# ScalarE's two output-side activations moved ahead of the next pair's two SiLUs, in every step of a hand-ordered Mamba-2 mixer

## The reference

```
x = x + block_sparse_linear(layernorm(x))
x = x + ffn(layernorm(x))        # gate/up/down weights dequantised from int4 values, SiLU gate
x = x + mamba2(layernorm(x))     # 128 heads of 64, state 128, 8 groups, chunks of 128
x = x + ffn(layernorm(x))
```

```
gate, hBC, dt = split(x @ in_proj_w.T)
hBC = silu(causal_conv4(hBC) + conv_b)            # x: 8192 channels, B and C: 1024 each
y   = ssm_scan(x, B, C, softplus(dt), A) + D * x
y   = y * rsqrt(mean(y*y) + eps) * norm_w * silu(gate)
out = y @ out_proj_w.T
```

## Time and profile before

| | |
|---|---|
| time, median of 3 runs | 2216.73 us (2215.08 to 2217.02) |
| the profiled execution, its own time | 2217.02 us |
| its span in the profile | 2215.3 us |
| mean granted TensorE clock | 0.982 of full speed |
| busy: TensorE, its weight loads | 96%, 79% of the span |
| busy: VectorE, ScalarE, GpSimd | 76%, 62%, 43% |

### The profile page before, as it was taken

One profiled execution on the slowest core, in us unless ns is written; L12 is line 12 of the kernel. 1 busy time (PEld: TensorE's weight loads), 2 busy tenths in 40 slices (PEclk: granted clock), 3 DMA queues, 4 the chain that ended last, 5 costly groups with the idle time before them and its releaser, 6 DMA issues. The chain is left out here.

```text
span 2215.3 us, 37449 instructions
## 1 busy us (share of the span) xinstructions
PE 2117.9 (96%) x13374; PEld 1740.4 (79%) x13374; DVE 1694.6 (76%) x2683; ACT 1378.9 (62%) x1872; POOL 944.2 (43%) x637
## 2 busy tenths in 40 slices
PE   5999976999999999999999999999999999859999
PEld 4788865788888888888888888888888888738887
DVE  8655566879888888878888888888888888665554
ACT  2222236787777877777787877777787777522221
POOL 2222222555454545454454555555454545342221
PEclk9999988999999999999999999999999999969999
DMA  4434313332323332333333333232333333333431
GB/s 166 131 128 169 105 59 100 98 113 93 118 91 111 101 106 99 109 97 109 97 108 97 109 97 114 92 118 87 112 98 103 103 107 98 119 110 118 170 140 68
DMA packets 128564, 241.89 MB, mean 109 GB/s; under 512 B 13968, under 2 KB 48528, under 8 KB 128144
## 3 DMA queue, kind: packets, MB, share of 16 engines
q1 hardware_dynamic: 128400, 239.73, 33.6%
HBM read 234.17 MB, written 5.51 MB: 108 GB/s over the span
## 5 line engine op out<-in xcount | busy, mean ns | idle before, releaser
L854 PE MATMUL ring<-m_lnt,w_sb 128*128 128x512 f32 x3456 | 857.3, 398 | 3.4 <-DVE xc L1196 3.4
L854 PEld LDWEIGHTS ring<-m_lnt,w_sb 128*128 128x128 f32 x3456 | 631.8, 189 | 127.9 <-DVE xc L1196 3.7
L1375 POOL TENSOR_TENSOR w_sb<-w_raw,w_sb 128x512 fp32r<-128x512 f32 x288 | 426.7, 1487 | 136.4 <-ACT w_sb L1050 136.1
L1390 POOL TENSOR_TENSOR ysq<-ysq,y 128x512 f32<-128x512 f32 x126 | 163.9, 1301 | 662.0 <-ACT y L1094 662.0
L951 PE MATMUL ring<-wo,ygs 128*128 128x512 f32 x1536 | 370.2, 390 | 2.2 <-POOL wo L1380 2.2
L951 PEld LDWEIGHTS ring<-wo,ygs 128*128 128x128 f32 x1536 | 287.7, 188 | 64.5 <-issue 4.3
L1196 DVE SCALAR_TENSOR_TENSOR xc<-ring,cw,xc 128x511 f32<-128x511 f32 (+2 forms) x384 | 286.1, 745 | 22.7 <-ACT xc L1062 13.6
L1380 POOL TENSOR_TENSOR wo<-wo_raw,wo 128x512 fp32r<-128x512 f32 x128 | 221.3, 1729 | 0.6 <-ACT wo L1106 0.6
L1050 ACT ACTIVATE w_sb<-w_raw 128x512 fp32r<-128x512 f32 x288 | 177.2, 621 | 55.7 <-DMA w_raw<-w_in 55.7
L1062 ACT ACTIVATE xc<-ring,cb,cw 128x512 f32<-128x512 f32 x128 | 99.2, 775 | 151.9 <-PE ring L854 151.9
L932 PE MATMUL yt<-em,x_dt 128*64 128x128 f32 x2048 | 184.2, 279 | 6.3 <-DVE state L1238 6.3
(11 more groups left out here) (182 smaller groups left out, 3192.9 us busy)
## 6 DMA issues: line engine op xcount, KB each, us to landing
w_raw<-w_in SPq DMA_DIRECT2D x288, 256.0 KB, 3.9
ce<-e_t SPq DMA_DIRECT2D x128, 384.0 KB, 4.1
wo_raw<-w_out SPq DMA_DIRECT2D x128, 256.0 KB, 4.4
f_gu_q<-gu_w SPq DMA_DIRECT2D x28, 512.0 KB, 5.2
f_gu_zr<-gu_z SPq DMA_DIRECT2D x28, 512.0 KB, 6.8
f_gu_sr<-gu_s SPq DMA_DIRECT2D x28, 512.0 KB, 8.1
f_dn_q<-dn_w SPq DMA_DIRECT2D x28, 256.0 KB, 7.0
f_dn_zr<-dn_z SPq DMA_DIRECT2D x28, 256.0 KB, 8.1
```

Source lines behind the costliest of these rows:

```text
L854: mm = nc.tensor.matmul(dst[:], w_sb[:, u % WR, wp, k * P:(k + 1) * P], lnt[:, xp, k, b * S:(b + 1) * S], start=(i == 0), stop=(i == 3 * K ...
L1375: nc.gpsimd.tensor_tensor(w_sb[:, u % WR, 1], w_raw[:, u % NR], w_sb[:, u % WR, 0].bitcast(F32), ALU.subtract).then_inc(w_lo, 1)
L1390: nc.gpsimd.tensor_tensor(part, part, y[:, k % 2], ALU.add).then_inc(ysq_done, 1)
```

## The change

In ScalarE's program for a step, `y_high(k - 1)` and `square(k - 1)` are put ahead of `activate_x(k + 1)` and `activate_z(k + 1)`. Nothing is added or removed, and no other engine's program changes. `y_high` waits for `yg_done`, the end of VectorE's `gate(k - 1)` of the same step.

```diff
                     for n in gram_in(k):
                         copy_btok(n)
+                    if 1 <= k <= K:
+                        y_high(k - 1)
+                        square(k - 1)
                     if k + 1 < K:
                         activate_x(k + 1)
                         activate_z(k + 1)
-                    if 1 <= k <= K:
-                        y_high(k - 1)
-                        square(k - 1)
                     for unit in ahead[2:]:
                         w_high(unit)
```

## The result

The changed kernel takes 2228.39 us (median of 6 runs, 2226.12 to 2231.49); the kernel before, in the runs beside it, 2216.26 (6 runs). The ratio is 1.0061, 95% interval 1.0050 to 1.0073: slower by 12.1 us. The forecast was 2229 us, a range of 2220 to 2241, and slower with a chance of 0.83. The profiled execution took 2228.82 us, 11.8 more than the one of before.

What follows compares the result with a forecast made beforehand. TensorE was taken to bound the kernel, busy 99.8% of the mixer's steady part. Fourteen steps at 0.74 us (10.4) plus 2 us of run-up gave 12.4 us on 2217.02, so 2229 us, range 2220 to 2241.

Steps and rivals of the forecast that it cites:

- The place: 14 steps with k mod 8 = 4 (12 to 116): TensorE waits for z's bank, about 0.74 us each; other steady steps about nothing.
- The chain: ScalarE from the gate's end through y_high, square, table load and SiLU(x) to SiLU(z)'s end: 3.60 us.
- The loads: ScalarE's table loads stay two a step, 255 in all; lost overlap adds 0.10 us, or 0 if y_high does not wait.
- Rival E: ScalarE drains before the moved load, up to 1.28 us more in each of 14 stalls: 18 more, 2247 us; chance 0.02.
- The relief: GpSimd's low copies come earlier, shortening VectorE's y_low and ce: 0.68 us back per k mod 8 = 4 step, bounds 0 and 1.35.
- the price of 1.42: Mean TensorE stall in each of the 14 k mod 8 = 4 steps, restart included, before anything is given back; 19.9 us together.
- The run-up: Start of the mixer, chiefly step 4: tap, convolution and SiLU of B and C 1.8 us later; 2 us, bounds 0 and 4.
- A: No measurable change: in the 14 steps the gate comes early enough to free z's bank; 2218 to 2221 us; chance 0.13.
- B: No relief: GpSimd's work slides from one VectorE instruction to another, 14 waits of 1.4 us; 2239 us; chance 0.15.
- D: Faster: an earlier y_high lets VectorE's chain start earlier in the run-up, where TensorE idles 19 us; 2211 us; chance 0.04.
- C: Further TensorE waits in ordinary steps, 0.1 us in each of 110, or its clock falls; 2240 to 2250 us; chance 0.09.
- hardly before the tap: Sign expected in the profile: ScalarE waits before y_high in nearly every step, 0.6 to 3.7 us, hardly before the tap.

Runs made afterwards that it cites:

- kernel 1: The changed kernel, but with the old order in the 16 steps with k mod 8 = 4; 2215.36 us, ratio 0.9993.
- kernel 2: The kernel before, but with the new order only in the 15 steps with k mod 8 = 4 from step 12 on; 2233.99 us, ratio 1.0084.
- 4: The changed kernel, but with SiLU(x) ahead of y_high and square, SiLU(z) behind them, in all steps; 2212.97 us, ratio 0.9991.
- 7: The changed kernel plus one unused activation behind square in the 14 steps with k mod 8 = 4 from step 12 on; 2235.87 us, ratio 1.0090.
- kernel 3: The kernel before, but with the new order in the steps with k mod 8 = 3 or 4 from step 11 on; 2226.93 us, ratio 1.0053.
- 8: kernel 2 with GpSimd's sum_squares cut to one column in the steps with k mod 8 = 3 from step 11 on; 2226.32 us, ratio 1.0055.
- 5: The changed kernel, but with SiLU(z) ahead of y_high and square, SiLU(x) behind them, in all steps; 2213.44 us, ratio 0.9989.
- 9: The kernel before, but with SiLU(z), y_high, square, SiLU(x) in that order in steps 0 to 4 alone; 2213.50 us, ratio 0.9989.

## Why the prediction was right, by its own steps

**The place.** The 14 steps with k mod 8 = 4 were to lose, the others not. Shown by kernels 1 and 2. One further step, 99, with k mod 8 = 3, waited too: 0.29 us by its row, and the step became 0.53 us longer. The prediction allowed such a step a cost if its gate came late. The gate did come 1.0 us late, but the Exp ended later still: ScalarE itself was late, by a wait of 3.52 us for a weight tile (row below).

**The chain.** 3.60 us forecast from the gate to the end of SiLU(z), 3.61 or 3.62 measured in each of the 14 steps. That both the wait and what stands behind it matter is shown by kernels 4 and 7.

**The loads.** 255 as before, and the load begins 0.02 us behind the square and not over it, the 0.10 us that was added. From the load's start to SiLU(z)'s end it is again 2.41 us. The drain of 1.38 us that the Trainium skill names (ScalarE: Activation LUTs, "What ACT_TABLE_LOAD costs") is not seen here either: from the load's end at 1009.04 to SiLU(x) at 1009.05 there is none, and the square's end at 1007.74 is 0.02 us ahead of the load. Rival E is out.

**The relief.** In step 52 the rows moved as worked out. Counted from the states before them, `wo_low` ends where it was forecast (994.6 on the clock of before), `w_low` runs 995.5 to 996.8, and `ce` starts at 996.0. `y_low` gave back 0.45 us and `ce` 0.27, where 0.45 and 0.2 were forecast, so the slip is 0.71, where 1.41 was worked out without relief. Over the 14 steps the loss was 11.1 us, 0.79 each, where 0.74 was forecast. That is a relief of 0.63 against the price of 1.42 that was read from before's rows, and of 0.51 against kernel 2, which lost 1.30.

That the mean came so close is partly luck. In ten of the 14 steps kernel 2 lost 1.51 on average and the changed kernel 0.75, a relief of 0.76: price and relief were both forecast too low there, by about the same. In steps 12, 92 and 116 there was nothing to give back: kernel 2 lost 0.48 to 0.68 there and the changed kernel 0.69 or 0.70. For step 12 the prediction had worked out 1.63 from before's rows, without seeing that the order of two starts 0.05 us apart decides it (experiment 2). And in step 100 the relief failed. In step 99 ScalarE waited for a late weight tile, so that the low copies of GpSimd came late too, `y_low` and `ce` took 1.47 and 1.93 us, and in step 100 the wait is the longest, 1.27 us. ScalarE in step 99, VectorE in step 100, TensorE behind it:

```profile
1584.51 0.63 ACT L1050 ACTIVATE w_sb<-w_raw 128x512 fp32r<-128x512 f32 x1 [3.52 <-DMA w_raw<-w_in]
```

```profile
1595.32 1.47 DVE L1277 TENSOR_TENSOR ygs<-sz,ygs 128x512 fp32r<-128x512 f32 x1
...
1597.31 1.93 DVE L1250 TENSOR_TENSOR ce<-ce,bc 128x768 f32<-128x768 f32 x1
```

```profile
1607.64 0.73 PE L854 MATMUL ring<-m_lnt,w_sb 128*128 128x512 f32 x2 [1.27 <-ACT sz L1072]
```

The forecast's 14 x 0.74 = 10.4 us came to 11.6 in the profile (11.1 in the 14 steps and 0.5 in step 99) and 11.2 in kernel 3.

**The run-up.** Forecast +2; the one profile says +2.4, and TensorE's wait for SiLU of B and C grew by 1.8 us as computed (0.7 to 2.5). But kernels 2 and 8 show 62 us of run-up with the old order. The term was of the right size beside the one profile of before, and is not shown to be the order's cost on average; steady stretch alone, the total would have been 11.6 of the 12.1 measured.

**The rivals.** A (the gate early enough) did not come about in any of the 14; B is kernel 2; D was half right about its place: orders exist that gain in the run-up (4, 5 and 9), but not this one. C is out by kernel 1, and the clock did not fall.

**Signs and reasons that failed.** ScalarE was to wait "hardly before the tap"; it waits there 106 times, 0.84 us on average (1.41 before). Its waits for the gate reach 5.5 us, not 3.7. And GpSimd's wait for `square` does not end 2.4 us sooner "in every step", as B's reason has it: ahead of `sum_squares` it fell from 5.41 to 3.00 us in step 51, but was 6.81 in both kernels in step 52, where ScalarE waits for the gate in either order. None of this enters the sum.

## What to carry to other kernels

A reordering on an engine with over a fifth of its time to spare can still be paid in full, if behind the moved instruction stands the last reader of a buffer that the bound engine wants back. Look up, for each step of the period, which release comes next to its deadline (here 2 steps of 8, by the rotation of three banks), not for the average step. And when an engine off the path is done sooner, ask on whom its follower's work falls: here 7.0 of the 18.2 us that kernel 2 lost were given back by GpSimd moving out of VectorE's way, set off in the step before.

## What the runs showed of the hardware that was not expected

TensorE's idle time before a matrix product understates a stall: in step 52 the product's row says 0.46 us, the weight load's row 0.65, and the slip of the step is 0.71. Over the steady stretch the 15 waits add up to 8.2 us by the first measure, while 11.6 were lost; the start-to-start distance is the number to use.

Where VectorE and GpSimd meet on 128x512 or 128x768 tensor operations, it can be either that is drawn out. In step 12 `ce` took 2.06 us and the copy 1.29 when the copy started 0.05 us ahead, and 0.94 and 2.10 when it started 0.01 us ahead. Two such pairs are too few for a rule, but the difference was worth about a microsecond of TensorE's time.
